# Q of two blocks by seven half-size products, with the mixed weights built in steps 7 to 14

## The chip, the cores and the metric

The kernel runs on one core of one Trainium2 chip. The metric is the device time of one execution in microseconds, as the median of several runs. Engines are named as in the profile: PE is TensorE (PEld its weight loads), DVE is VectorE, ACT is ScalarE, POOL is GpSimd, SP is SyncE, whose queue (SPq) issues every DMA here.

## What is computed

A gated cross-attention layer followed by a gated quantised linear layer, on 2048 tokens of width 512 (32 sequences of 64):

```
xn = layernorm(x)
Q = xn @ Wq.T          # 32 heads of 128
K, V = ctx @ Wk.T, ctx @ Wv.T      # 8 heads of 128, four query heads share one
P = softmax(causal(Q K^T / sqrt(128)))
x = x + tanh(g0) * ((P V) @ Wd.T)
x = x + tanh(g1) * (layernorm(x) @ dequantise(qweight).T + bias)
```

All matrix products run in f16 with each operand split in a high and a low half (HI, LO), in three passes, HI*HI, HI*LO and LO*HI.

## The kernel before, in words

The tokens form 4 blocks of 512 (`BLOCKS`, index tb), the heads 8 groups of 4 (`GROUPS`, index g). A step n = 8*tb + g, 32 in all, does the attention of one group on one block; within step n the products Q, K and V of step m = n + 1 are made too. On PE a step is written out by hand: the two score units of n, then `q_unit(m, 0..3)` (each 4 chunks of the contraction x 3 passes = 12 matmuls of 128x512), `p_transpose(n, 0)`, `k_unit(m)`, `p_transpose(n, 1)`, half of `v_unit(m)`, `av_unit(n, 0)`, `av_unit(n, 1)`, the rest of `v_unit`, then `y_unit(n, 0)`, `av_unit(n, 2)`, `y_unit(n, 1)`, `av_unit(n, 3)`, `y_unit(n, 2)`, `y_unit(n, 3)`. Steps 11 and 19 also hold four `ffn_unit`s between the Q units.

PSUM has eight banks: `pa` (2) for Q, K, V, `py` (2) for the output product, `av` (2), `ps` and `pp`. Q units alternate between the two `pa` banks, so `q_unit(m, 2)` and `(m, 3)` wait until ACT has written the HI half of the unit two before (L677) and DVE the LO half (L897, in `lo_part`). Each engine executes its own list in order, so DVE's list for a step matters: scores(n, 0), q_part 0, scores(n, 1), normalise(n, 0), q_part 1, p_part 0, normalise(n, 1), q_part 2, p_part 1, q_part 3, k_part, av_part 0 and 1, v_part, and then for j = 0 to 3: y_part(n, j) (L976, adds the output product to `xacc`), av_part(j + 2) for j < 2, and what belongs to a layernorm (`ln_bn`, `ln_stats`, `ln_norm`) or the linear layer (`ffn_zero`, `ffn_weight`) in that step.

Weights: in block 0 they are read in f32, split into HI and LO (ACT, DVE, and POOL for K, V and the output weights) and kept in DRAM (`kept_q` and so on); from step 8 on they come back from there into two buffers (`back_qkv`), the output weights `wd` into a single buffer (`back_d(n)`, which waits until the output products of step n - 1 are done). SP's queue in a step n of blocks 1 to 3: `back_d(n)`, loads of the next block's x and context, `back_qkv(m + 1)`, then DMA transposes of normalised tiles from `xh` to `xT` (`transpose_tiles`, 16 a step in four or so steps of a block), `duplicate_v(m)` and stores. POOL makes the LO halves of normalised tiles (`ln_lo`), the Newton steps of a layernorm (`ln_rstd`), `residual` and `ffn_add`.

## Time and profile before

| | us |
|---|---|
| median of 3 runs | 1057.8 (1057.64 to 1058.18) |
| the profiled execution | 1056.85 |
| its span, first to last instruction | 1054.9 |
| PE busy | 1017.7 |
| DVE busy | 682.1 |
| ACT busy | 456.6 |
| POOL busy | 233.9 |

Times in the rows count from the first instruction. Busy time says how full an engine is; what sets the end is read from the chain of waits and from the time by time view of PE. Matmuls are pipelined, so the pitch of a matmul is read as the distance of starts, not from its duration.

### The profile page before, as it was taken

Reading aid. Unit: us, or ns where it says so; the run is one execution under the profiler, and the core shown is the slowest. Engines: PE = TensorE matmul, PEld = TensorE weight load, DVE = VectorE, ACT = ScalarE, POOL = GpSimd, SP = SyncE. Lnnn points to the kernel's source line nnn. Section 1 sums busy time; section 2 is a strip of 40 time slices with the busy share of each in tenths; the row PEclk is TensorE's granted clock in tenths of the full one; section 3 lists DMA queues with packets and bytes.
Section 4 is the critical chain, followed back from the end, with each engine's and each line's share of the span. In section 5 each row is a group of like instructions: output and inputs, shape, how many; then the busy total and the mean of one; then the engine's idle time right before and its main releaser. Section 6 shows DMA issues by size and latency. Waiting matters only on the chain.

```text
span 1054.9 us, 19976 instructions
## 1 busy us (share of the span) xinstructions
PE 1017.7 (96%) x7842; PEld 569.2 (54%) x7842; DVE 682.1 (65%) x1374; ACT 456.6 (43%) x917; POOL 233.9 (22%) x245
## 2 busy tenths in 40 slices
PE   5889999999999999999999999999999999999995
PEld 3455555555555555555555554555555555555542
DVE  6856677777577666765466556755556664555678
ACT  5767676676533243333334333244433322333322
POOL 1355565465604000210002100210000300000013
PEclk9999999999999999999999999999999999999998
DMA  7757645445355632345422743333432443224111
GB/s 278 235 153 272 216 163 182 161 135 157 102 178 196 149 90 66 141 133 137 132 71 70 206 134 121 109 119 93 131 122 108 133 137 126 62 86 143 64 36 60
DMA packets 90219, 142.61 MB, mean 135 GB/s; under 512 B 31248, under 2 KB 64016, under 8 KB 79504
## 3 DMA queue, kind: packets, MB, share of 16 engines
q1 hardware_dynamic: 90128, 141.34, 42.0%
q8 instruction: 64, 1.05, 0.4%
q14 instruction: 27, 0.22, 0.1%
HBM read 94.11 MB, written 25.17 MB: 113 GB/s over the span
## 4 chain that ended last, share of the span: by engine, by line
PE 87%; DVE 7%; ACT 3%; issue 2%; DMA 1%; SPq 0%; DVEq 0%; ACTq 0%
PE pa L1295 42%; PE py L1295 30%; PE av L1408 5%; PE pp L1391 3%; PE ps L1375 2%; PE py L1466 2%; PE pp L1375 2%; DVE q L897 1%; DVE sc L943 1%; DMA raw_q<-in_wqT 1%; DVE sc L954 1%; DVE row_max L941 1%; DVE sc L937 1%; ACT q L677 1%; PE av L1442 0%
## 5 line engine op out<-in xcount | busy, mean ns | idle before, releaser
L1295 PE MATMUL pa<-xT,wq 128*128 128x512 f16 x1536 | 342.7, 379 | 9.5 <-DVE q L897 6.7
L1295 PE MATMUL py<-wd,att 128*128 128x512 f16 x1488 | 336.2, 379 | 0.8 <-issue 0.8
L1295 PEld LDWEIGHTS pa<-xT,wq 128*128 128x128 f16 x1536 | 145.8, 98 | 189.9 <-issue 22.5
L1295 PEld LDWEIGHTS py<-wd,att 128*128 128x128 f16 x1488 | 143.3, 98 | 159.1 <-issue 1.1
L677 ACT ACTIVATE q<-pa 128x512 f16<-128x512 f32 x128 | 75.7, 591 | 264.3 <-PE pa L1295 264.3
L976 DVE SCALAR_TENSOR_TENSOR xacc<-py,f_y,xacc 128x512 f32<-128x512 f32 x128 | 95.7, 747 | 125.0 <-PE py L1295 124.9
L728 ACT ACTIVATE att<-av 128x256 f16<-128x256 f32 x256 | 80.8, 384 | 145.7 <-PE av L1408 145.2
L967 DVE SCALAR_TENSOR_TENSOR att<-av,att 128x256 f16<-128x256 f32 x256 | 93.3, 416 | 67.1 <-ACT att L728 66.9
L897 DVE SCALAR_TENSOR_TENSOR q<-pa,q 128x512 f16<-128x512 f32 x128 | 87.7, 685 | 57.0 <-ACT q L677 54.2
L1295 PE MATMUL pa<-wv,cT 128*128 128x128 f16 x1536 | 96.2, 219 | 0.0
L1295 PEld LDWEIGHTS pa<-wv,cT 128*128 128x128 f16 x1536 | 89.9, 98 | 0.9
L1295 PE MATMUL pa<-cT,wk 128*128 128x512 f16 x384 | 88.1, 379 | 1.6 <-DVE q L897 1.4
L1408 PE MATMUL av<-pT,v_dup 128*128 128x256 f16 x512 | 71.6, 272 | 0.1
L897 DVE SCALAR_TENSOR_TENSOR k<-pa,k 128x512 f16<-128x512 f32 x32 | 22.1, 692 | 70.9 <-ACT k L683 70.9
L717 ACT CAST pr<-sc 128x256 f16<-128x256 f32 x64 | 32.6, 510 | 79.3 <-DVE sc L954 79.1
L721 ACT COPY pT<-pp 128x1024 f16<-128x1024 f16 x64 | 64.4, 1006 | 4.7 <-PE pp L1391 4.2
L499 POOL TENSOR_SCALAR raw_d<-raw_d,w_mul 128x512 f32<-128x512 f32 x32 | 54.3, 1697 | 21.9 <-ACT wd L672 21.9
L1295 PEld LDWEIGHTS pa<-cT,wk 128*128 128x128 f16 x384 | 36.0, 98 | 41.6 <-issue 3.3
L1408 PEld LDWEIGHTS av<-pT,v_dup 128*128 128x128 f16 x512 | 48.3, 99 | 16.7 <-issue 0.3
L556 POOL TENSOR_TENSOR xacc<-xacc,xn 128x512 f32<-128x512 f32 x8 | 10.1, 1268 | 179.7 <-DVE xacc L1104 179.7
L522 POOL TENSOR_TENSOR xh<-xn,xh 128x512 f16<-128x512 f32 x26 | 29.5, 1165 | 75.7 <-ACT xh L701 75.7
L556 POOL TENSOR_TENSOR xacc<-xacc,raw_q 128x512 f32<-128x512 f32 x4 | 5.0, 1268 | 183.6 <-DVE raw_q L1112 183.6
(131 smaller groups left out, 1060.1 us busy)
## 6 DMA issues: line engine op xcount, KB each, us to landing
wq<-kept_q SPq DMA_DIRECT2D x24, 1024.0 KB, 7.1
wd<-kept_d SPq DMA_DIRECT2D x23, 1024.0 KB, 4.8
v_dup<-v_nat SPq DMA_DIRECT2D x128, 128.0 KB, 2.4
raw_d<-in_wdT SPq DMA_DIRECT2D x8, 1024.0 KB, 10.1
kept_q<-wq SPq DMA_DIRECT2D x8, 1024.0 KB, 8.8
kept_d<-wd SPq DMA_DIRECT2D x8, 1024.0 KB, 5.4
raw_q<-in_wqT SPq DMA_DIRECT2D x7, 1024.0 KB, 5.6
wk<-kept_k SPq DMA_DIRECT2D x24, 256.0 KB, 7.3
```

The costliest lines, as they stand in the source:

```text
L499: pool.tensor_scalar(raw, raw, scale, None, ALU.mult).then_inc(w_scaled, 1)
L677: act.activation(q[:, HI, :, :, h, :], pa[h % 2][:, :].rearrange("p (b u s) -> p b u s", b=BPB, u=HALVES), ACT.Copy, scale=Q_SCALE).then_i ...
L717: act.copy(pr[:, p, :, HI, 0:keys(p)], sc[:, p, :, 0:keys(p)]).then_inc(p_hi, 1)
L721: act.copy(pT[:, :, :, p * HQ:(p + 1) * HQ], pp[:, :].bitcast(F16).rearrange("p (b h s) -> p b h s", b=BPB, h=HPG)).then_inc(pT_ok, 1)
L728: last = act.activation(att[:, HI, :, at:at + S], av[j % 2][:, bb * 256:(bb + 1) * 256].rearrange("p (h s) -> p h s", h=HPG), ACT.Copy, sc ...
L897: dve.scalar_tensor_tensor(out=out, in0=in0, scalar=scale, in1=hi, op0=ALU.mult, op1=ALU.subtract).then_inc(done, 1)
L967: last = dve.scalar_tensor_tensor(out=att[:, LO, :, at:at + S], in0=av[j % 2][:, bb * 256:(bb + 1) * 256].rearrange("p (h s) -> p h s", h= ...
L976: dve.scalar_tensor_tensor(out=acc(t), in0=py[j % 2][:, :], scalar=f_y[:, n:n + 1], in1=acc(t), op0=ALU.mult, op1=ALU.add).then_inc(y_ok, 1)
L1295: last = pe.matmul(out, stationary(a, i), moving(b, i), start=(i == 0 and (a, b) == PASSES[0]), stop=(i == count - 1 and (a, b) == PASSES[ ...
L1375: last = pe.matmul((pp, ps)[p][:, b * keys(p):(b + 1) * keys(p)], q[:, a, b, p, :, :].rearrange("p h s -> p (h s)"), k[:, c, b * S:b * S + ...
L1391: last = pe.transpose(bank16[:, b * P:(b + 1) * P], pr[:, p, b, :, :].rearrange("p c s -> p (c s)"), ident[:, :])
L1408: last = pe.matmul(av[j % 2][:, bb * 256:(bb + 1) * 256], v_dup[:, n % 2, b, c, :], pT[:, b, :, :].rearrange("p h s -> p (h s)"), start=(c ...
```

## The change

Blocks 2 and 3 (`fast(m)`, m = 16 to 31, so the Q work in steps n = 15 to 30) no longer multiply four heads one after the other. The 2x2 arrangement of two heads by two halves of the contraction, times two halves of the contraction by two halves of the tokens, is computed with Winograd's seven products. Each product `run(m, r, i)` (r: pair of heads, i = 1 to 7) is 2 chunks x 3 passes = 6 matmuls of 128x256. A step has 14 of them. Partial sums share banks: ACT copies three intermediate results out of PSUM (`copy_p1`, `copy_p5`, `copy_u2`), DVE adds three more to them (`add_11`, `add_22`, `add_12`), and the split in HI and LO is done by quadrants of 128x256.

Two sets of operands are new. The sums and differences of Wq (`ws`, kept in `kept_s`) are made one group a step in steps 7 to 14: a load of 1 MB from `in_wqT`, four tensor operations on POOL (`mix_weights`), four ACT and four DVE operations for HI and LO (`mix_hi`, `mix_lo`), and a store of 1 MB (`keep_mix`). In steps 15 to 29 `back_mix` brings them back. The sums and differences of the normalised tokens (`tT`) are made in steps 12 and 20 (`mix_norm`, `mixed_hi`, `mixed_lo`) and transposed by 32 DMA transposes in steps 13 and 14, and 21 and 22; 8 plain transposes drop out of each of these blocks' layernorms. To that end the layernorm of blocks 2 and 3 moves one step earlier (`norm_step` 3).

The last two output units of step n - 1 (`y_unit(n - 1, 2)` and `(n - 1, 3)`) move into step n between the half products for n = 15 to 30; `back_d(n)` then comes after `back_qkv`, `back_mix` and four transposes in SP's queue. In these steps `ffn_add` comes earlier on POOL, and the `ffn_zero` of the late tiles moves to after `k_part` in step 25. Small tiles share one buffer, and staging buffers are reused (`ff_raw`, `xs` and `th` in the K and V staging, `ff_int` and `ff_sum` single).

```diff
+        BANK_X, BANK_Y, BANK_Z = (pa[0], av[1]), (pa[1], pa[1]), (av[0], av[0])
...
+            def mix_weights(g):
+                pool.wait_ge(s_ld, 16 * (g + 1))
...
+                pool.tensor_tensor(a22, a22, a21, ALU.add).then_inc(s_mix, 1)
+                pool.tensor_tensor(a21, a11, a21, ALU.subtract).then_inc(s_mix, 1)
...
+                pool.tensor_tensor(a11, a22, a11, ALU.subtract).then_inc(s_mix, 1)
...
+                pool.tensor_tensor(a12, a12, a11, ALU.subtract).then_inc(s_mix, 1)
...
+                if mixing(n) is not None:
+                    pool.wait_ge(k_lo, n + 2)
+                    mix_weights(mixing(n))
```

ACT, in a fast step and, last, in steps 7 to 14:

```diff
+                if fast(m):
+                    copy_p1(m, 0)
+                    exp(n, 0)
+                    copy_p5(m, 0)
+                    copy_u2(m, 0)
+                    exp(n, 1)
+                    hi_11(m, 0)
+                    p_part(n, 0)
+                    hi_22(m, 0)
+                    hi_12(m, 0)
+                    copy_p1(m, 1)
...
+                    if mix_of(n) is not None:
+                        for t in range(TILES):
+                            mixed_hi(mix_of(n), t)
+                    if call is not None:
+                        for t in range(TILES):
+                            ln_hi(TILES * call + t, g == 0)
+                    continue
...
                 av_part(n, 2)
+                if mixing(n) is not None:
+                    mix_hi(mixing(n), (0, 1))
...
                 av_part(n, 3)
+                if mixing(n) is not None:
+                    mix_hi(mixing(n), (2, 3))
```

DVE:

```diff
+                if fast(m):
+                    scores(n, 0)
+                    scores(n, 1)
+                    add_11(m, 0)
+                    normalise(n, 0)
+                    add_22(m, 0)
+                    add_12(m, 0)
+                    lo_11(m, 0)
+                    lo_22(m, 0)
+                    lo_12(m, 0)
+                    normalise(n, 1)
+                    lo_21(m, 0)
+                    p_part(n, 0)
+                    y_late(2)
+                    p_part(n, 1)
+                    add_11(m, 1)
+                    y_late(3)
+                    add_22(m, 1)
+                    add_12(m, 1)
...
+                if mixing(n) is not None and j in (1, 2):
+                    mix_lo(mixing(n), 2 * j - 2)
+                    mix_lo(mixing(n), 2 * j - 1)
```

PE:

```diff
+                elif (r, i) == (1, 5):
+                    pe.wait_ge(c12_ok, pair_count(m, 0))
...
+                elif i == 6:
+                    pe.wait_ge(p1_ok, pair_count(m, r))
+                elif i == 7:
+                    pe.wait_ge(u2_ok, pair_count(m, r))
+                elif i == 3:
+                    pe.wait_ge(p5_ok, pair_count(m, r))
+                elif i == 4:
+                    pe.wait_ge(c22_ok, pair_count(m, r))
...
+                    elif i == 4:
+                        pe.wait_ge(t4_ld, 16 * 8 * (tb - FIRST_BLOCK + 1))
...
+                if fast(m):
+                    run(m, 0, 1)
+                    run(m, 0, 5)
+                    run(m, 0, 2)
+                    run(m, 0, 6)
+                    y_unit(n - 1, 2)
+                    run(m, 0, 7)
+                    run(m, 0, 3)
+                    run(m, 1, 1)
+                    run(m, 0, 4)
+                    run(m, 1, 5)
+                    run(m, 1, 2)
+                    run(m, 1, 6)
+                    y_unit(n - 1, 3)
+                    run(m, 1, 7)
+                    run(m, 1, 3)
+                    p_transpose(n, 0)
+                    run(m, 1, 4)
```

SP:

```diff
-                if GROUPS <= n < LAST:
+                if GROUPS <= n < LAST and not fast(m):
                     back_d(n)
...
                 if GROUPS <= m + 1 < STEPS:
                     back_qkv(m + 1)
-                if dma_tiles(n) is not None:
-                    transpose_tiles(*dma_tiles(n))
+                if fast(m + 1):
+                    back_mix(m + 1)
+                transpose_first(n)
+                if fast(m) and n < LAST:
+                    back_d(n)
+                transpose_rest(n)
                 if m < STEPS:
                     duplicate_v(m)
...
+                if mixing(n) is not None:
+                    keep_mix(mixing(n))
+                if mixing(n + 1) is not None:
+                    load_mix(mixing(n + 1))
```

## Rows read from the trace of the kernel before

**Rows 1.** The page, part 1: busy time of each engine.
```profile
PE 1017.7 (96%) x7842; PEld 569.2 (54%) x7842; DVE 682.1 (65%) x1374; ACT 456.6 (43%) x917; POOL 233.9 (22%) x245
```
**Rows 2.** The page, part 4: the chain that ended last, by engine.
```profile
PE 87%; DVE 7%; ACT 3%; issue 2%; DMA 1%; SPq 0%; DVEq 0%; ACTq 0%
```
**Rows 3.** Stretches: length, then PE, PEld, DVE, ACT, POOL busy. Step 17, step 19.
```profile
579.12:609.39 30.27, 30.22 (x238) 16.96 (x237) 16.93 (x32) 9.66 (x20) 6.02 (x5) 1.00 0.69 192
639.65:676.98 37.33, 37.33 (x274) 20.58 (x273) 23.77 (x51) 9.88 (x20) 3.42 (x3) 1.00 0.28 99
```
**Rows 4.** Time by time, PE in step 18: start, length, line, operation.
```profile
609.39 0.76 PE L1375 MATMUL pp<-k,q 128*128 128x32 f16 x24
...
610.69 10.74 PE L1295 MATMUL pa<-xT,wq 128*128 128x512 f16 x48
621.26 0.61 PE L1391 MATMUL pp<-ident,pr 128*128 128x128 f16 x8
...
626.09 1.04 PE L1408 MATMUL av<-pT,v_dup 128*128 128x256 f16 x8
626.96 1.50 PE L1295 MATMUL pa<-wv,cT 128*128 128x128 f16 x24
628.42 2.75 PE L1295 MATMUL py<-wd,att 128*128 128x512 f16 x12
631.01 0.60 PE L1408 MATMUL av<-pT,v_dup 128*128 128x256 f16 x4
```
**Rows 5.** Groups of instructions: count, busy us, mean ns of one, idle before.
```profile
L967 DVE SCALAR_TENSOR_TENSOR att<-av,att 128x256 f16<-128x256 f32 x256 | 93.3, 416 | 67.1 <-ACT att L728 66.9
L728 ACT ACTIVATE att<-av 128x256 f16<-128x256 f32 x256 | 80.8, 384 | 145.7 <-PE av L1408 145.2
L897 DVE SCALAR_TENSOR_TENSOR wq<-raw_q,w_mul,wq 128x512 f16<-128x512 f32 x32 | 31.0, 1003 | 0.2
L897 DVE SCALAR_TENSOR_TENSOR wk<-raw_k,w_mul,wk 128x512 f16<-128x512 f32 x1 | 0.8, 751 | 0.0
```
**Rows 6.** Time by time, DVE in step 18.
```profile
614.11 0.69 DVE L897 SCALAR_TENSOR_TENSOR q<-pa,q 128x512 f16<-128x512 f32 x1 [2.47 <-ACT q L677]
614.71 0.74 DVE L937 SCALAR_TENSOR_TENSOR sc<-ps,f_score,mask 128x512 f32<-128x512 f32 x1
...
616.82 0.41 DVE L950 TENSOR_REDUCE row_sum<-sc 128x8 f32<-128x256 f32 x1
...
617.85 0.68 DVE L897 SCALAR_TENSOR_TENSOR q<-pa,q 128x512 f16<-128x512 f32 x1
...
618.93 0.69 DVE L950 TENSOR_REDUCE row_sum<-sc 128x8 f32<-128x512 f32 x1
...
620.50 0.68 DVE L897 SCALAR_TENSOR_TENSOR q<-pa,q 128x512 f16<-128x512 f32 x1
```
**Rows 7.** Time by time, DVE and POOL in steps 8 and 9.
```profile
305.90 0.69 DVE L943 TENSOR_TENSOR sc<-sc,row_max 128x512 f32<-128x512 f32 x1
...
336.16 1.28 DVE L943 TENSOR_TENSOR sc<-sc,row_max 128x512 f32<-128x512 f32 x1
...
331.76 5.14 POOL L550 TENSOR_TENSOR xacc<-xacc,ff_rows 128x512 f32<-128x512 f32 x4 [1.48 <-DVE ff_rows L1096]
```
**Rows 8.** Time by time, DVE in step 10 (its first score matmul is at 360.19).
```profile
364.92 0.69 DVE L897 SCALAR_TENSOR_TENSOR q<-pa,q 128x512 f16<-128x512 f32 x1 [0.22 <-ACT q L677]
```
**Rows 9.** Time by time, POOL in steps 8 and 11.
```profile
319.65 0.20 POOL L543 TENSOR_TENSOR rstd<-rs_t,rs 128x4 f32<-128x4 f32 x1
...
421.96 1.27 POOL L556 TENSOR_TENSOR xacc<-xacc,xn 128x512 f32<-128x512 f32 x1 [85.06 <-DVE xacc L1104]
```
**Rows 10.** SP's queue: 16 transposes of step 18; the reload of `wd`, us to landing.
```profile
611.68 20.97 SPq L400 DMA_TRANSPOSE xT<-xh  x16
...
wd<-kept_d SPq DMA_DIRECT2D x23, 1024.0 KB, 4.8
```
**Rows 11.** Time by time, ACT at the end of step 20: HI halves of a layernorm.
```profile
702.80 2.19 ACT L701 ACTIVATE xh<-xn 128x512 f16<-128x512 f32 x4
```

More of the change, by code:

```diff
@@ L26 @@
 STEPS = BLOCKS * GROUPS
+HB = BT // 2
+HK = D // 2
 HI, LO = 0, 1
@@ L568, in _ @@
                     split_wv(1)
+                if mix_of(n) is not None:
+                    mix_norm(mix_of(n))
                 if call is not None:
                     ln_rstd(call)
+                if ffn_of(n) is not None and fast(n + 1):
+                    for t in range(ffn_of(n) * TILES, (ffn_of(n) + 1) * TILES):
+                        ffn_add(t)
                 if tb == 0:
@@ L579, in _ @@
                         residual(t)
-                if ffn_of(n) is not None:
+                if ffn_of(n) is not None and not fast(n + 1):
                     for t in range(ffn_of(n) * TILES, (ffn_of(n) + 1) * TILES):
@@ L821, in _ @@
                     ctx_squares(tb + 1, squares_done(g + 2) + 2 if tb == 0 else squares_done(GROUPS))
+                if mix_of(n) is not None:
+                    for t in range(TILES):
+                        mixed_hi(mix_of(n), t)
                 if call is not None:
@@ new lines, in _ @@
+                if fast(m):
[12 more added lines that the diff above has]
+                    y_late(2)
+                    p_part(n, 1)
+                    add_11(m, 1)
+                    y_late(3)
+                    add_22(m, 1)
+                    add_12(m, 1)
+                    lo_11(m, 1)
+                    lo_22(m, 1)
+                    lo_12(m, 1)
+                    lo_21(m, 1)
+                    if ffn is not None:
+                        ffn_scaled(t0)
+                    k_part(m)
+                    if g == 1 and tb == BLOCKS - 1:
+                        for t in LATE:
+                            ffn_zero(t)
+                    if ffn is not None:
+                        ffn_scaled(t0 + 1)
+                        ffn_scaled(t0 + 2)
+                    if call is not None and g == 0:
+                        ln_stats(call)
+                    av_part(n, 0)
+                    av_part(n, 1)
+                    if ffn is not None:
+                        ffn_scaled(t0 + 3)
+                    v_part(m)
+                else:
+                    scores(n, 0)
+                    if n == 0:
+                        for h in range(2, HPG):
+                            split_wq(1, h)
+                    q_part(m, 0)
+                    scores(n, 1)
+                    normalise(n, 0)
+                    q_part(m, 1)
+                    if n == 0:
+                        weight_scale(1, slice(3, 4))
+                        step_factors(n)
+                    if ffn is not None:
+                        ffn_scaled(t0)
+                    p_part(n, 0)
+                    normalise(n, 1)
+                    q_part(m, 2)
+                    if ffn is not None:
+                        ffn_scaled(t0 + 1)
+                    p_part(n, 1)
+                    q_part(m, 3)
+                    if ffn is not None:
+                        ffn_scaled(t0 + 2)
+                        ffn_scaled(t0 + 3)
+                    k_part(m)
+                    if call is not None and g == 0:
+                        ln_stats(call)
+                    av_part(n, 0)
+                    av_part(n, 1)
+                    v_part(m)
@@ L1204, in _ @@
                 for j in range(TILES):
-                    if n < LAST - 1:
+                    if n < LAST - 1 and not (deferred(n) and j >= 2):
                         y_part(n, j)
@@ L1220, in _ @@
                         ffn_zero(t0 + j)
-                    if g == 1 and tb == BLOCKS - 1:
-                        ffn_zero(LATE[j])
                     if prep:
```

458 lines of the change are left out of this document (365 added, 93 removed).

## The prediction

> **What bounds the kernel now.** I read the busy shares first: PE 1017.7 of 1054.9 us, DVE 65% [rows 1]. The chain of waits says the same, 87% on PE [rows 2]. Then the stretches of one step: an ordinary step of blocks 1 to 3 takes 30.27 us of which PE is busy 30.22, and step 19, with the linear layer, 37.33 of 37.33 [rows 3]. So a microsecond of matmul taken out is a microsecond gained, as long as no wait takes its place. The time by time view gives the pitches [rows 4]. A 12-matmul unit of 128x512 takes 631.01 - 628.42 = 2.59 us, 216 ns each; eight of 128x256 take 626.96 - 626.09 = 0.87 us, 109 ns each. Four Q units would be 4 x 2.59 = 10.36; they take 621.26 - 610.69 = 10.57. The missing 0.21 is a wait: `q_unit(m, 3)` needs the LO half of unit 1, which DVE finishes at 617.85 + 0.68 = 618.53 [rows 6], 9.14 after the step's start at 609.39, when unit 3 is due at 9.07. DVE is thus level with PE in the first third of each step, although it is busy only 16.93 of 30.27 us [rows 3]. What it has in reserve is the 2.47 us idle before 614.11 [rows 6].
>
> **What the change removes.** Per fast step 48 matmuls at 10.57 us become 14 x 6 = 84 at 109 ns = 9.16 us: 1.41 us less. 16 steps (n = 15 to 30), of which step 19 has no 0.21 wait: 22.4 us. The pitch is from the `av` product, the same form (f16, 128x256, weights changed at every matmul), so I see no reason for another. From a page of the Trainium skill another sum would follow: TensorE: Matmul & The Clock Gate, Back-to-back issue gap, states a sustained spacing of about 81 ns at 128 columns and 131 at 512, with weight loads in the stream; by it (an estimate, midway in columns some 98 ns) 84 short products would cost more than 48 long ones, 8.2 against 6.3 us, and the change would lose. The trace disagrees at both ends I can read, 216 ns at 512 and 109 at 256 [rows 4], and the measurement decides.
>
> **The ordinary fast step, placed by hand.** Half product = 0.66 us. From the step's start on PE: scores to 1.30; products 1, 5, 2 to 3.27, 6 to 3.92; y2 to 6.51; 7 and 3 to 7.82; 1' to 8.48; 4 to 9.13; 5', 2', 6' to 11.10; y3 to 13.69; 7', 3', the transpose to 15.44; 4' to 16.10. The rest is as before, so the step ends at 28.86. DVE starts its scores at 1.6, later than before, since av_part(3) (ends 1.65) no longer has y2 and y3 behind it. scores 0 takes 1.4, scores 1 616.82 - 614.71 = 2.11, an addition like one L967 0.36 to 0.42, normalise 0 617.85 - 616.82 = 1.03 [rows 5, 6]: idle at 6.45. Product 7 is read at 7.37, `add_22` is done at 7.75, product 4 wants it at 8.48. DVE may be 1.5 us late there. Second chain: `add_12` 8.40, three LO quadrants at 0.36, normalise 1 620.50 - 618.93 = 1.57, lo_21, p_part 0, y2 (0.7), p_part 1, `add_11'` end near 13.3; y3 arrives at 13.9, `add_22'` is done at 14.95, wanted at 15.44. So 0.3 us is spare after y3 and 0.6 before. ACT's eight quadrants and six copies at 0.38 [rows 5] fit: `copy_u2'` done at 13.0, wanted at 13.69. I take 0 for the ordinary step, with 0 to 0.5 as bounds (the upper if each of the 10 additions and LO quadrants in the chain takes 0.42 with gaps, not 0.36). Nothing hides more than that.
>
> **Where waits appear: fast steps.**
> - Steps 15 and 23, first products on a new block. One DMA transpose holds SP's queue 20.97 / 16 = 1.31 us [rows 10]. Step 22 has 4 + 16 of them, step 21 as many, steps 13 and 14 20 each. Adding up SP's queue (reloads 2.1, four transposes 5.3, `back_d` held until y3 at 13.9, 16 x 1.33, the V copies 2.6), step 22 begins at 9.1 in its own time, and the last transpose is issued at 9.1 and lands at 10.6 in step 23, where product 4 wants it at 8.5: 2.1 us. By the same sum step 15 waits 1.4. Bounds 0 and 5 together.
> - Step 22: `back_d` issued at 16.9 lands 4.8 later [rows 10] at 21.7, wanted at 22.8; beside transposes it may take 7: 0.5 taken, 0 to 1.5.
> - Steps 17, 21, 25: four ACT operations on layernorm tiles take 2.19 to 2.6 us [rows 11]; they now come after av_part(3) (0.86) with no y2 and y3 as cover and ahead of `copy_p1`, done then at 3.7 for a product 6 due at 3.27: 0.6 each.
> - Step 20: step 19's DVE list ends with ctx, four normalisations, four `ffn_zero` (0.7 each), so its scores start 3.1 us late, 1.6 over what is spare, and POOL's `ffn_add` beside it: 2.1. Steps 16, 24 (two statistics around y3) 0.3 each; step 19 0.2; step 25, four `ffn_zero` ahead of av_part: 0.7.
> Sum: 1.4 + 2.1 + 0.5 + 1.8 + 2.1 + 0.6 + 0.2 + 0.7 = 9.4, bounds 3 and 18.
>
> **Where waits appear: steps 7 to 14.** POOL's four operations of one group are 4 x 1.3 = 5.2 us [rows 9], the DVE's four between 0.75 and 1.0 each [rows 5]; no POOL work lies beside them, so 0.75 with overlap, 2.7 us. After y1 and y2 DVE has about as much idle time, so in steps 7, 13 and 14 this costs nothing (if the 1.0 held, 1 us each). It isn't free where the list is full:
> - Step 8: POOL ends the Newton steps at 319.85 [rows 9], and only then mixes, to 325.3. ACT waits for that ahead of av_part(3), so DVE has it at 328.3, and y3 due at 326.74 waits: 1.7 us.
> - Step 9: POOL's `residual` moves later over DVE's scores. With POOL active, L943 takes 1.28 in place of 0.69 [rows 7]: 0.6 more. So says a rule of the Trainium skill too (SBUF — State Buffer, Who interferes with whom): DVE with two SBUF inputs and a reading GpSimd exclude each other; the trace agrees with its 1.28.
> - Step 10: the first Q part on DVE came at 364.92 with 0.22 idle before it [rows 8]. To the `ffn_weight` work of step 9 come the 2.7 and, by the earlier layernorm, two statistics (1.3). DVE's Q part 0 ends 8.0 into the step where unit 2 is due at 6.5 (1.5), and part 1 ends at 11.8 for unit 3 at 10.6 (1.2): 2.5 more than now.
> - Step 11, with its four linear units as cover: 0.4. Steps 11 and 12: `ln_norm` before y1, then `ffn_add` and `mix_norm` of POOL (eight operations at 1.27) over DVE's scores: 1.5.
> Sum 6.7, bounds 2 and 11. The DMA traffic, some 32 MB more, stays behind other work: the loads are issued most of a step ahead.
>
> **The sum.** 22.4 - 9.4 - 6.7 = 6.3 us. The profiled span of 1054.9 becomes 1048.6; 1.95 lies around it in that execution (1056.85), and the median is another 0.95 higher: 1057.8 - 6.3 = 1051.5.
>
> **The rivals.**
> - The waits overlap. A step in which PE waited gives DVE, SP and POOL time too, so the waits of neighbouring steps aren't a sum. With the lower bounds 3 and 2 the gain is 17.4: 1040.4. For it: 8 of my 11 fast waits are under 1 us. Against: those of steps 8, 10, 20, 23 have different causes. Chance 0.22, within 1040 to 1048.
> - SP's queue. 20 transposes take 26 us of a 28.9 us step, and if transposes slow down beside the 1 MB loads, `back_d` and the last transposes are late in all steps with transposes, ten steps at 0.5 to 1 us: gain near 0, 1056 to 1060. Against: in step 18 wq, wk, wv and 16 transposes ran together at 1.31. Chance 0.15.
> - The other side: DVE sets the pace of the fast steps. Mechanism: the wait of product 4' for `add_22'`, behind everything DVE does between y2 and y3. It decides from 0.3 us of lateness on; if additions and quadrants take 0.48 and each semaphore hop 0.1 more, lateness is 1 to 1.5 a step, 16 to 24 us: 1061 to 1075. For it: DVE rises from 17 to about 20 us busy in a step of 28.9, and the present 0.21 wait shows how it gets level with PE. Against: L967's pairs show 0.36. It turns into a loss at 0.4 us a step. Chance 0.15.
> - The half products don't get the pitch per column: a cost per matmul, and not per column, holds them, say at 160 ns, halfway between 109 and 216. Then 84 x 0.16 = 13.4 us, 2.9 more than now in each of 16 steps, and with the 16 us of waits 1120. The `av` row speaks against it [rows 4]. Chance 0.02; the page of the Trainium skill named above points this way.
>
> **How the numbers follow.** Forecast 0.46 (gain 3 to 10, 1048 to 1055). About 0.2% is what a measurement of this kernel tells from no change. Faster: 0.46 + 0.22 and some of the queue case, 0.70. Same: most of the queue case, 0.14. Slower: 0.15 and 0.02 less rounding, 0.16. The range from 1040 to 1060 leaves out the DVE case and the weight loads; within it lie 8 in 10.
>
> **What would show it.** Right: 84 half products at 109 ns in 9.2 us of PE; ordinary steps 26 to 30 of 28.9 us; waits of PE above 1 us only in steps 8, 10, 12, 15, 20 and 23, the last on DMA. Wrong: a DVE wait before product 4' in every fast step, steps 13 and 14 longer than 30.3, or `wd` as a releaser of y0. If all of 22 us arrives, my DVE lateness is overestimated; if step 30 isn't shorter than 29.5, the pitch or the ordinary step is wrong.

## The result and the profile after

The changed kernel takes 1075.6 us (median of 4 runs, 1073.5 to 1076.3), the kernel before 1058.0 beside it: ratio 1.0162, interval 1.0144 to 1.0180. It is slower by 1.6%, where 1051.5 was forecast and 1060 was the upper end. The profiled execution of the changed kernel took 1073.51, its span is 1071.7.

The page of the changed kernel: the span, part 1 (busy us, share, instructions), the granted clock in 40 slices, and the chain that ended last.

```profile
span 1071.7 us, 22269 instructions
...
PE 1005.0 (94%) x8418; PEld 626.8 (58%) x8418; DVE 757.7 (71%) x1566; ACT 522.4 (49%) x1117; POOL 307.8 (29%) x293
...
PEclk9999999999999999999989999999999999999998
...
PE 63%; DVE 16%; SPq 10%; ACT 4%; issue 4%; DMA 2%; DVEq 0%; ACTq 0%
```

PE lost only 12.7 us of busy time against [rows 1], although 22.4 us of matmul went. Some of its matmuls ran at a lower clock (5.2 us in steps 12, 15 and 22, below), and busy time grows a little in a step that waits even at the full clock: 29.39 us in step 17 for the 28.86 of step 18. The chain fell from 87% on PE [rows 2] to 63%; 16% now is DVE and 10% SP's queue, which had 0%.

The next view gives stretches: length, then PE, PEld, DVE, ACT, POOL busy with counts, granted clock, DMA share, GB/s. Steps 17 and 18.

```profile
593.84:624.72 30.88, 29.39 (x275) 20.39 (x273) 22.57 (x44) 14.61 (x38) 10.68 (x8) 1.00 0.64 203
624.72:653.58 28.86, 28.86 (x274) 20.55 (x272) 20.61 (x46) 12.30 (x30) 0.00 (x0) 1.00 0.52 164
```

Step 18 takes 28.86 us, all of it PE, where it took 30.27 [rows 3]: that is the forecast for an ordinary fast step, to the hundredth. The 22.4 us therefore did arrive. Step 17, with POOL at work for 10.7 us, takes 2.0 more. So I compared the length of each step (from score start to score start) with its length without waits. Those are 30.27 for a step of blocks 1 to 3, 28.86 for a fast one, 37.32 for step 11, 36.14 for step 19, in which the trace shows no wait, and 25.09 for step 14, whose last two output units went into step 15. Step 9 is compared with its 30.85 in the kernel before, as the forecast did. A measured wait contains the lower clock behind it.

| waits, us | forecast | measured |
|---|---|---|
| step 8 | 1.7 | 1.4 |
| step 9 | 0.6 | 1.8 |
| step 10 | 2.5 | 2.6 |
| step 11 | 0.4 | 0.3 |
| step 12 | 1.5 | 4.7 |
| step 14 | 0 | 0.6 |
| step 15 | 1.4 | 11.1 |
| step 17 | 0.6 | 2.0 |
| step 20 | 2.1 | 3.8 |
| step 22 | 0.5 | 5.9 |
| step 23 | 2.1 | 1.3 |
| step 25 | 1.3 | 3.0 |
| steps 16, 19, 21, 24 | 1.4 | 0.7 |
| sum | 16.1 | 39.2 |

39.2 less 22.4 is a loss of 16.8 us, as the two spans have it; the medians show 17.6. Of the 23.1 us by which the waits exceed the forecast, 9.7 are one step. PE in step 15 (its scores start at 524.73), time by time: start, length, and in brackets the idle time before and its releaser.

```profile
526.75 0.82 PE L1768 MATMUL pa<-xT,wq 128*128 128x256 f16 x6 [0.56 <-issue]
528.65 0.81 PE L1768 MATMUL pa<-raw_q 128*128 128x256 f16 x6 [1.08 <-DMA raw_q<-raw_kv]
...
534.51 0.82 PE L1768 MATMUL av<-xT,wq 128*128 128x256 f16 x6
542.12 1.44 PE L1768 MATMUL pa<-raw_q,wq 128*128 128x256 f16 x6 [6.79 <-DMA raw_q<-raw_kv]
543.35 1.49 PE L1768 MATMUL pa<-raw_q 128*128 128x256 f16 x6
544.63 1.49 PE L1768 MATMUL av<-xT,wq 128*128 128x256 f16 x6
545.91 0.89 PE L1768 MATMUL av<-raw_q 128*128 128x256 f16 x6
```

`raw_q<-raw_kv` is a mixed transpose. PE waits 6.79 us for the last of them, and the three products behind the wait come 1.23, 1.28 and 1.28 us apart, while the others keep 0.655. The granted clock of that stretch (542.12 to 545.91) is 0.50, which is the 1.2 GHz level in place of 2.4; it costs another 1.9 us. After it, it is 1.00 again. SP's queue of the same stretch:

```profile
439.10 5.08 SPq L561 DMA_DIRECT2D out_x<-xacc  x4
...
448.89 20.97 SPq L477 DMA_TRANSPOSE xT<-xh  x16
469.95 3.10 SPq L453 DMA_DIRECT2D v_dup<-v_nat  x4
...
478.26 10.07 SPq L477 DMA_TRANSPOSE xT<-xh  x8
488.51 16.71 SPq L489 DMA_TRANSPOSE raw_q<-raw_kv  x12
505.32 2.60 SPq L453 DMA_DIRECT2D v_dup<-v_nat  x4
...
513.82 27.02 SPq L489 DMA_TRANSPOSE raw_q<-raw_kv  x20
```

The 56 transposes take 74.8 us, 1.34 each, and with what stands between them the queue works from 444 to 541 with no gap above 0.6 us. Before that its stores wait for POOL's `ffn_add`. Step 22 shows the same queue with the reload of `wd` in it: SP first, then PE.

```profile
765.04 5.04 SPq L489 DMA_TRANSPOSE raw_d<-raw_kv  x4
770.17 0.53 SPq L440 DMA_DIRECT2D wd<-kept_d  x1
770.81 23.66 SPq L489 DMA_TRANSPOSE raw_d<-raw_kv  x16
```
```profile
778.30 4.36 PE L1693 MATMUL py<-wd,att 128*128 128x512 f16 x12 [4.23 <-DMA wd<-kept_d]
795.70 0.82 PE L1768 MATMUL pa<-raw_d,wq 128*128 128x256 f16 x6 [1.10 <-DMA raw_d<-raw_kv]
```

The reload is issued at 18.95 us of the step and is usable 8.1 us later, beside transposes that take 1.48 each. The 12 matmuls behind the wait take 4.36 us in place of 2.75, again at the lower clock level for most of it (granted 0.59 from 778.30 to 782.30).

My theory after this reading: some 18 us are SP's queue, which the mixed transposes fill (step 15, 22, 23), and the rest are DVE: operations with two operands in SBUF slowed by POOL, and lists that are too long in steps 8 to 12. The rivals are named with each run.

### The profile page after: what moved, and what is told of

Same layout as the page of the kernel before. It is cut to its first block, busy times and chain, and to the rows that moved or that the text cites. A ratio compares the mean times of both kernels' runs of the same rounds, so it can differ in the third digit from the quotient of the medians.

```text
span 1071.7 us, 22269 instructions
## 1 busy us (share of the span) xinstructions
PE 1005.0 (94%) x8418; PEld 626.8 (58%) x8418; DVE 757.7 (71%) x1566; ACT 522.4 (49%) x1117; POOL 307.8 (29%) x293
## 4 chain that ended last, share of the span: by engine, by line
PE 63%; DVE 16%; SPq 10%; ACT 4%; issue 4%; DMA 2%; DVEq 0%; ACTq 0%
PE py L1693 23%; PE pa L1693 20%; SPq L489 8%; PE pa L1768 5%; PE av L1872 4%; PE av L1768 4%; DVE q L1194 2%; PE pp L1850 2%; PE py L1930 2%; SPq L477 1%; PE ps L1834 1%; DVE xacc L1323 1%; PE pp L1834 1%; DVE xacc L1451 1%; DVE sc L1290 1%
## 5 line engine op out<-in xcount | busy, mean ns | idle before, releaser
L1693 PE MATMUL py<-wd,att 128*128 128x512 f16 x1488 | 340.7, 380 | 7.9 <-DMA wd<-kept_d 5.0
L1693 PE MATMUL pa<-xT,wq 128*128 128x512 f16 x768 | 173.6, 381 | 15.8 <-DVE q L1194 13.9
L1693 PEld LDWEIGHTS pa<-xT,wq 128*128 128x128 f16 x768 | 72.9, 98 | 107.9 <-issue 25.8
L871 ACT ACTIVATE q<-pa 128x512 f16<-128x512 f32 x64 | 37.7, 589 | 81.7 <-PE pa L1693 81.7
L738 POOL TENSOR_TENSOR xacc<-xacc,raw_kv 128x512 f32<-128x512 f32 x12 | 17.6, 1482 | 207.8 <-DVE raw_kv L1463 177.0
L915 ACT COPY pT<-pp 128x1024 f16<-128x1024 f16 x64 | 64.2, 1003 | 4.7 <-PE pp L1850 4.2
L687 POOL TENSOR_TENSOR small<-rs 128x4 f32<-128x4 f32 x18 | 4.6, 258 | 210.3 <-DVE rs L1348 209.4
L1872 PEld LDWEIGHTS av<-pT,v_dup 128*128 128x128 f16 x512 | 48.3, 99 | 16.9 <-issue 0.3
L907 ACT ACTIVATE sc<-sc 128x256 f32<-128x256 f32 x64 | 33.4, 521 | 45.4 <-DVE sc L1290 45.4
L1194 DVE SCALAR_TENSOR_TENSOR q<-pa,q 128x512 f16<-128x512 f32 x64 | 43.7, 683 | 13.1 <-ACT q L871 12.5
```

Of the source, the lines that this page charges most:

```text
L871: act.activation(q[:, HI, :, :, h, :], pa[h % 2][:, :].rearrange("p (b u s) -> p b u s", b=BPB, u=HALVES), ACT.Copy, scale=Q_SCALE).then_i ...
L907: act.activation(sc[:, p, :, 0:keys(p)], sc[:, p, :, 0:keys(p)], ACT.Exp).then_inc(exp_ok, 1)
L915: act.copy(pT[:, :, :, p * HQ:(p + 1) * HQ], pp[:, :].bitcast(F16).rearrange("p (b h s) -> p b h s", b=BPB, h=HPG)).then_inc(pT_ok, 1)
L1194: dve.scalar_tensor_tensor(out=out, in0=in0, scalar=scale, in1=hi, op0=ALU.mult, op1=ALU.subtract).then_inc(done, 1)
L1693: last = pe.matmul(out, stationary(a, i), moving(b, i), start=(i == 0 and (a, b) == PASSES[0]), stop=(i == count - 1 and (a, b) == PASSES[ ...
L1872: last = pe.matmul(av[j % 2][:, bb * 256:(bb + 1) * 256], v_dup[:, n % 2, b, c, :], pT[:, b, :, :].rearrange("p h s -> p (h s)"), start=(c ...
```

## Experiments

**The mixed transposes left out.** Left out are the 64 transposes and all waits for them; the seven products read the plain tokens, so Q comes out wrong, but PE's work is the same. If the queue is the cause, the 64 transposes alone explain steps 15, 22 and 23; the rival is DVE.

```diff
             def transpose_mixed(tb, some):
 
+                return
...
-                b = xT[:, par, :, :, :] if i in (1, 2, 3) else tT[par]
+                b = xT[:, par, :, :, :]
```

> Left out: the 64 DMA transposes of the mixed tokens (32 for each of blocks 2 and 3) and the waits for them; the seven products read the plain tokens instead, so their values are wrong but their work is the same. Theory A (SP's queue is the cause of the DMA waits): in the changed kernel's trace step 15 is 11.1 us, step 22 5.9 and step 23 1.3 longer than the 28.86 of an ordinary fast step, 18.3 in all, with the transposes' wait (6.8 + 1.1), the reload of wd (4.2) and a lower clock behind them. All of it goes: 1075.6 - 18.3 = 1057, steps 15, 22 and 23 between 28.9 and 30. Rival B (DVE is late there too, the wait on DMA only covers it): step 15 starts with DVE 2.7 us late from the weights' LO parts, and at least 1.2 us of step 15 stay; if the DVE is worse than that, steps 15 and 23 stay above 31 and the time is 1062 to 1070.

Measured: 1056.5 us, ratio 0.9983 (0.9971 to 0.9996). Step 15 takes 29.86, steps 22 and 23 take 28.87 and 28.86, step 14 takes 25.09; all others are as in the changed kernel, to 0.04. In step 15 one wait is left:

```profile
535.11 0.83 PE L1767 MATMUL pa<-xT,wq 128*128 128x256 f16 x6 [0.68 <-DVE junk L1231]
```

The loads of the mixed weights are still in the queue here. So the mixed transposes cost 19.1 us by the medians and 17.9 by the four steps, as waits and by the clock behind them. Without any of them the change gains only 1.5 to 2 us of 22.4: the other half of the loss is elsewhere.

**The stores a step later.** The queue's long run begins with four stores that wait for POOL's `ffn_add`. If they move behind the transposes, these start earlier.

```diff
-                if ffn_of(n) is not None:
-                    for t in range(ffn_of(n) * TILES, (ffn_of(n) + 1) * TILES):
+                if n > 0 and ffn_of(n - 1) is not None:
+                    for t in range(ffn_of(n - 1) * TILES, (ffn_of(n - 1) + 1) * TILES):
                         store(t)
```

> Same work; the four stores of steps 11 and 19 stand one step later in SP's queue, behind the transposes of steps 12 and 20. Theory A: in step 12 the queue then waits only for the weights' LO parts (ready at 439.6) and its transposes start 4.6 us earlier, in step 20 about 6 us earlier. Of step 15's wait of 6.8 about 2.2 is left and its lower clock goes, step 22's wait of 4.2 for wd goes, together 10 to 12 us less: 1064. Rival C (the queue is full anyway, 20 transposes a step at 1.33, so it catches up with the same lateness): no more than 3 us less, 1073.

Measured: 1074.5 us, ratio 1.0152 (1.0123 to 1.0182). My expectation of 1064 fell and the rival's 1073 held. This execution's step 12 starts at 435.88, the changed kernel's at 433.79, so times are compared from there. The 16 transposes start 10.2 us into step 12 in place of 15.1: the head start of 4.9 us that I expected was there. The next row of transposes starts only 2.0 us earlier (42.5 in place of 44.5), since the four stores, 2.2 us of queue, now stand between them.

```profile
446.11 21.05 SPq L477 DMA_TRANSPOSE xT<-xh  x16
467.26 2.60 SPq L453 DMA_DIRECT2D v_dup<-v_nat  x4
469.90 2.16 SPq L561 DMA_DIRECT2D out_x<-xacc  x4
...
478.39 10.07 SPq L477 DMA_TRANSPOSE xT<-xh  x8
```

The last 20 end 104.9 us after the start of step 12 in place of 107.1. PE still waits 6.63 us for them, and steps 14 and 15 together are 1.6 us shorter, while 22 and 23 are 0.6 longer. Reordering alone mends little in a full queue.

**One part alone, twice.** First the weights are mixed, stored and fetched by nobody, and Q is made as before (no fast step, no sums of the tokens). Then the reverse: seven half products in the fast steps, but no sums of weights; they read the plain weights.

```diff
         def fast(m):
-            return FIRST_FAST <= m < STEPS
+            return False
```

> Q of all blocks by whole heads as before; kept from the change: the sums and differences of the weights in steps 7 to 14 (made and stored, never used) and the layernorm one step earlier; left out: the mixing of tokens. Theory A: steps 8 to 12 cost what they cost in the changed kernel, 1.4 + 1.8 + 2.6 + 0.3 and of step 12's 4.7 perhaps 3 (the token sums on POOL are missing), so 9 us over before: 1067, and steps 13 to 30 at 30.3. Rival D (this work is hidden behind PE and the cost sits in the fast steps): within 2 us of 1057.8.

```diff
         def mixing(n):
...
-            return g if 0 <= g < GROUPS else None
+            return None
```

> The fast steps and the mixing of tokens as changed; left out: the sums and differences of the weights in steps 7 to 14, their loads and stores; the second set of weights comes back from the plain kept weights, so the values are wrong. Theory A: steps 8 to 11 return to the lengths of before (30.3, 30.9, 30.3, 37.3; 6 us less), step 12 keeps a part of its 4.7 (POOL's additions beside DVE's scores; 1 to 2 left), and SP's queue reaches step 15 some 5 us less late, 5 to 7 us less there: 1075.6 - 6 - 3 - 6 = 1060.6. Rival D: the first steps stay as long and only fast steps change: above 1068.

Measured: 1069.2 (1.0102, 1.0073 to 1.0132) and 1057.1 (0.9995, 0.9980 to 1.0011). With the weights mixed alone steps 8 to 12 take 31.69, 32.64, 32.88, 37.66 and 34.85, the same as in the changed kernel to 0.15; from step 13 on all but steps 20 and 25 are 30.27 or 37.32. Step 12's wait was the surprise: I had put it down to the sums of the tokens, and it is there without them. Without the mixing, steps 8 to 12 are 30.28, 30.86, 30.28, 37.32 and 31.02, and step 15 waits 2.6 us for a transpose in place of 6.8:

```profile
527.74 0.82 PE L1767 MATMUL pa<-raw_q,wq 128*128 128x256 f16 x6 [2.59 <-DMA raw_q<-raw_kv]
```

The queue's transposes begin 10.0 us into step 12 in place of 15.1, and from the first of them to the end of the last it needs 86.4 us in place of 92.0, with the loads and stores of the mixed weights gone from it. PE, whose step 12 is 4.0 us shorter, takes back a part of this. Steps 22 and 23 together are 65.54 us, against 64.93 with the mixing: in those steps there are no such loads and stores in either kernel, and the queue is just as late.

**POOL's additions made narrow.** `residual` and `ffn_add` work on 4 columns of 512, so that POOL is busy for much less time at the same places. The rest of the output then lacks the bias and the linear layer's result. If contention on SBUF is the cause, steps 9, 12, 17, 20 and 25 get shorter; if DVE's lists are too long, nothing does.

```diff
-                pool.tensor_tensor(acc(t), acc(t), part, ALU.add).then_inc(out_pool, 1)
+                pool.tensor_tensor(acc(t)[:, 0:4], acc(t)[:, 0:4], part[:, 0:4], ALU.add).then_inc(out_pool, 1)
```

> As the changed kernel, but POOL's residual and ffn_add work on 4 of 512 columns, so the bias and the linear layer's result are missing from the rest of the output; all instructions, their order and waits stay. Theory A (DVE operations with two operands in SBUF are held up by POOL's): steps 9, 12, 17, 20 and 25 were 1.4 + 1.8, 4.7, 2.0, 3.8 and 3.0 over their length without waits; step 17 falls to 0.5, step 12 to 2, step 20 to 2.6, step 25 to 1.5, step 9 by 0.5: some 8 us less, and the stores, done sooner, let SP's queue start 5 us earlier in steps 12 and 20, worth 1 to 3 more: 1065. Rival B (DVE's own list is too long there, POOL is no part of it): at most 1 us less in these steps: 1073 or more.

Measured: 1060.0 us, ratio 1.0015 (1.0000 to 1.0029). Step 9 0.8 shorter, 12 0.9, 17 1.6, 20 1.7, 25 1.7. DVE and POOL in step 17 of the changed kernel, and then DVE at the same place with narrow additions:

```profile
602.57 1.03 DVE L1194 SCALAR_TENSOR_TENSOR q<-p,q 128x256 f16<-128x256 f32 x1
603.52 2.89 DVE L1194 SCALAR_TENSOR_TENSOR q<-junk,q 128x256 f16<-128x256 f32 x2
```
```profile
600.57 5.56 POOL L732 TENSOR_TENSOR xacc<-xacc,ff_rows 128x512 f32<-128x512 f32 x4
```
```profile
600.75 0.42 DVE L1194 SCALAR_TENSOR_TENSOR q<-p,q 128x256 f16<-128x256 f32 x1
601.09 0.75 DVE L1194 SCALAR_TENSOR_TENSOR q<-junk,q 128x256 f16<-128x256 f32 x2
```

A LO quadrant takes 0.42 us alone and 1.03 to 1.45 beside POOL. The seven products copy partial results to SBUF, so three of the four quadrants now have both operands there; before, the split read Q from PSUM. That is how the change made DVE more sensitive to POOL. The form with an operand in PSUM isn't slowed: `q<-pa,q`, of twice the width, keeps its 0.68 in the middle of POOL's 437.37 to 443.83.

```profile
442.63 0.68 DVE L1194 SCALAR_TENSOR_TENSOR q<-pa,q 128x512 f16<-128x512 f32 x1
```

The steps give 6.8 us in all, the span 12.0. Step 22 gains 4.7 us and step 23 waits 4.7 longer, so the two together stay at 64.92: when `wd` comes sooner, PE meets the same late transposes one step later. As for the span, the other 5.2 lie behind the start of step 31, where the last linear layer's own `residual` and `ffn_add` are narrow too (50.0 us to the end in place of 55.3). That part says nothing on the change. The medians differ by 15.6, of which the profiled executions show 11.3; the rest is the spread between executions.

**The LO halves of the mixed weights by ACT.** It takes the four `mix_lo` a step off DVE. What ACT writes is the scaled weight, not its LO half.

```diff
-                        mix_lo(mixing(n), 2 * j - 2)
-                        mix_lo(mixing(n), 2 * j - 1)
...
+                    for h in range(HPG):
+                        act.activation(ws[mixing(n) % 2][:, LO, h, :, :], raw_s[:, h, :].rearrange("p (k n) -> p k n", k=KC),
+                                       ACT.Copy, scale=w_mul[:, mixing(n), 0:1]).then_inc(s_lo, 1)
```

> As the changed kernel, but in steps 7 to 14 the LO parts of the mixed weights are written by ACT as plain copies behind the HI parts (their values are wrong), and DVE has none of these four operations a step. Theory A (step 10's 2.6 us are DVE's list: mix_lo 2.7 us and two more statistics behind the linear weights): step 10 falls to within 0.5 us of 30.27, step 9 from 32.6 to 31, step 12 from 35.0 to 33, step 8 stays at 31.7, as it hangs on POOL and ACT: 6 us less: 1069. Rival C (the earlier layernorm and POOL make these steps long): steps 9, 10 and 12 shrink by under 1 us together, 1074.

Measured: 1072.0 us, ratio 1.0126 (1.0101 to 1.0151). Step 10 falls from 32.88 to 30.28 and step 11 to 37.32: there it is DVE's list. Step 12 falls by 2.4 of its 4.7. Step 14 takes 32.12, since `wd` comes 5.2 us late, and step 15 2.7 less. Step 9 became longer (33.50 in place of 32.63). The trace shows how: ACT's four extra operations (2.55 us) delay its HI halves of the layernorm, so POOL's `ln_lo` starts 0.65 us into step 9, where it had started 1.80 before it, and the last row of `ffn_rows` on DVE takes 1.64 us in place of 0.68:

```profile
335.17 1.64 DVE L1446 SCALAR_TENSOR_TENSOR ff_rows<-ff_rows 128x512 f32<-128x512 f32 x1
```
```profile
332.52 5.32 POOL L670 TENSOR_TENSOR xh<-xn,xh 128x512 f16<-128x512 f32 x4 [6.26 <-ACT xh L895]
```

DVE's list of step 11 in the changed kernel, POOL beside it, and what PE makes of it:

```profile
431.61 3.22 DVE L1194 SCALAR_TENSOR_TENSOR raw_q<-raw_d,w_mul,raw_q 128x512 f16<-128x512 f32 x2
...
436.31 3.31 DVE L1194 SCALAR_TENSOR_TENSOR raw_q<-raw_d,w_mul,raw_q 128x512 f16<-128x512 f32 x2
```
```profile
431.28 6.12 POOL L670 TENSOR_TENSOR xh<-xn,xh 128x512 f16<-128x512 f32 x4 [6.37 <-ACT xh L895]
437.37 6.46 POOL L738 TENSOR_TENSOR xacc<-xacc,raw_kv 128x512 f32<-128x512 f32 x4
```
```profile
443.45 7.05 PE L1693 MATMUL pa<-xT,wq 128*128 128x512 f16 x24 [3.02 <-DVE q L1194]
```

A `mix_lo` takes 1.6 us here; two take 1.41 where POOL is still, as at 395.36. The four cost 6.5 us, not 2.7, ahead of step 12's scores on DVE. PE waits 3.02 us, and the 24 matmuls behind the wait take 6.89 us to the next start in place of 24 x 0.216 = 5.18: step 12's 4.7 us are 3.0 of wait and 1.7 of lower clock (granted 0.75 over the 24). No single edit took all of it away: without `mix_lo` 2.3 us are left, with narrow additions 3.8.

**Half of the mixed transposes by PE.** The tiles 0 and 1 are transposed by PE in 2 x 8 short matmuls and copied out by ACT; SP keeps 32 of 64. All of the work is done.

```diff
+                for c in (HI, LO):
+                    for i in range(KC):
+                        at = (c * KC + i) * P
+                        last = pe.transpose(bank16[:, at:at + P], th[:, t, c, i * P:(i + 1) * P], ident[:, :])
+                last.then_inc(tm_mm, 1)
```

> Complete work. Of the 32 DMA transposes of mixed tokens in each of blocks 2 and 3, the 16 of the first two tiles are done on PE (8 transposes into one av bank and one ACT copy, one tile in each of steps 13, 14, 21 and 22). Theory A (SP's queue, at 1.32 us a transpose, is what makes steps 15, 22 and 23 long): without all 64 the kernel took 1056.5; 32 fewer take 21 us off the queue in each block, more than the 8 us that it was late, so the DMA waits go as they did there, and PE gains 4 x 0.45 us of work: 1058.5, step 15 at 29.9, steps 22 and 23 at 28.9 (step 22 29.3). Rival C (the queue stays full, since reloads and V copies wait on one another in it): a wait on DMA above 1 us is left in step 15 or 22: 1061 or more.

Measured: 1060.3 us, ratio 1.0019 (1.0006 to 1.0031). Steps 15, 22 and 23 take 29.87, 30.01 and 28.87. The 32 transposes taken over cost PE 0.45 us in each of four steps, and the kernel gains 15.3 us net. This settles the queue: with the same data by another way its loss is all but gone.

**POOL and stores a step later as well.** To the last kernel are added: the stores a step later; `residual`, `ffn_add` and the sums of the tokens later on POOL, behind the last LO quadrants; `mix_hi` after av_part 3; the late `ffn_zero` in step 26.

```diff
-                if g == 0 and tb > 0:
+                if g == 1 and tb > 0:
+                    pool.wait_ge(k_lo, n + 2)
                     for t in range((tb - 1) * TILES, tb * TILES):
                         residual(t)
```

> Complete work: the former kernel, and POOL's and ACT's work put where DVE is not in its first third. residual a step later and behind k_part; ffn_add in the step after, behind k_part (its stores a step later too); the token sums of step 12 behind the fourth Q unit; the HI parts of the mixed weights behind av_part 3; the late ffn_zero in step 26. Theory A (placement of POOL beside DVE's scores and LO quadrants): of the former's waits step 8's 1.4, 1.2 of step 9, 3 of step 12, 2.0 of step 17, 1.5 of step 20, 2.5 of step 25 go, 11 us: 1047 to 1049, faster than the kernel before. Rival B (the waits hang on the length of DVE's list, not on POOL): 1055 or more.

Measured: 1055.5 us, ratio 0.9957 (0.9941 to 0.9973), faster than both kernels but 6 us short of my expectation. The profiled execution is the slowest of the seven (1059.0, the fastest took 1053.7), so a fall of the clock that it shows need not be in the median. Steps 12, 17 and 25 take 32.27, 29.22 and 29.23, as wanted. Three places didn't follow. Step 8 stayed at 31.70, so the order on ACT, my mechanism of the prediction, wasn't its cause. Step 20 stayed at 32.72; DVE and POOL ahead of its scores, then PE:

```profile
682.08 4.00 DVE L1467 SCALAR_TENSOR_TENSOR xacc<-ff_rows,small,xacc 128x512 f32<-128x512 f32 x3
```
```profile
681.25 5.84 POOL L671 TENSOR_TENSOR xh<-xn,xh 128x512 f16<-128x512 f32 x4 [30.42 <-ACT xh L897]
```
```profile
688.42 1.08 PE L1783 MATMUL pa<-raw_q,raw_d 128*128 128x256 f16 x6 [2.02 <-ACT junk L945]
```

And step 22 took 33.04, for `wd` stands behind four transposes; behind a wait of 1.99 us the clock was at the lower level (granted 0.57 from 767.05 to 771):

```profile
767.05 4.45 PE L1708 MATMUL py<-wd,att 128*128 128x512 f16 x12 [1.99 <-DMA wd<-kept_d]
```

**Room for DVE in three places.** One edit for each of these.

```diff
+                if mixing(n) == 1:
+                    pool.wait_ge(q_lo, 4 * n + 8)
+                    mix_weights(1)
                 if call is not None:
                     ln_rstd(call)
...
-                transpose_first(n)
+                if fast(m) and g != 6:
+                    transpose_first(n)
                 if fast(m) and n < LAST:
                     back_d(n)
+                if not fast(m) or g == 6:
+                    transpose_first(n)
...
+                    if g == 2 and tb == 2:
+                        ffn_zero(4 + j)
```

> The complete work, as in the kernel of e8 (half of the mixed transposes by PE, stores and three of POOL's lists a step later), with three more edits, each against one wait that was left there. (1) Step 8: POOL makes the sums of the weights of group 1 ahead of the norm's reciprocal roots, from the moment when the last quadrant of Q is written, and not beside DVE's four ln_norm. Theory (two engines on SBUF operands slow each other, ln_norm 0.91 each in place of 0.48): the four take 1.91 us again and step 8 goes from 31.70 to 30.3. Rival (the engines aren't what slows it, DVE's list is too long): 31.7 stays. (2) Step 20's start: the four ffn_zero of block 1 go from step 19 to step 18, so that they don't lie beside POOL's ln_lo ahead of the scores; theory: step 20, which was 32.72 with 2.0 of wait and a fall of the clock behind it, takes 29.0 to 29.5; rival: the scores of step 20 stay late by DVE's ln_norm, 31 or more. (3) Step 22: SP issues the reload of wd ahead of four transposes (4.98 us of its queue) and no longer behind them; theory: the wait of 1.99 us on wd and the half clock behind it go, step 22 from 33.04 to 29.9; rival (the transfer is slowed by the transposes behind it, wherever it stands): 31.5 to 33. Sum by the theory 1.4 + 3.4 + 3.1 = 7.9 us under e8's 1055.5: 1047.6, range 1046 to 1050, ratio to the kernel before 0.990. If all three rivals hold: 1054 or more.

Measured: 1049.1 us (5 runs, 1047.0 to 1050.3), ratio 0.9914 (0.9900 to 0.9927). Step 8 takes 31.04, step 22 29.36 and step 20 28.90; step 9 took 32.22, 0.4 more. The profiled execution is the fastest of its five, that of the kernel with POOL and stores later the slowest of its seven: they differ by 12 us and the medians by 6.3, so the steps overstate what the three edits give. Of the 3.8 us of step 20, 1.75 came back in step 19 (37.90), where DVE is now late with the scores: the four `ffn_zero` take 3.0 us of its list wherever they stand. The four `ln_norm` of step 8, first in the changed kernel beside POOL's sums, then in this one, where POOL has ended by 317.4:

```profile
322.56 3.65 DVE L1400 TENSOR_SCALAR xn<-xacc,mv,small 128x512 f32<-128x512 f32 x4
```
```profile
322.34 1.26 POOL L702 TENSOR_TENSOR raw_d<-raw_d 128x512 f32<-128x512 f32 x1
323.69 1.33 POOL L704 TENSOR_TENSOR raw_d<-raw_d 128x512 f32<-128x512 f32 x1
```
```profile
323.13 1.91 DVE L1422 TENSOR_SCALAR xn<-xacc,mv,small 128x512 f32<-128x512 f32 x4
```
```profile
316.14 1.27 POOL L708 TENSOR_TENSOR raw_d<-raw_d 128x512 f32<-128x512 f32 x1
```

With that the 1.27 us wait of step 8 is gone. The 0.77 us that are left are a new one: POOL's sums now lie beside DVE's short operations of `ln_stats`, one of which takes 1.24 us in place of 0.17, and PE's first output unit waits for av_part 1 behind them:

```profile
316.19 1.24 DVE L1367 TENSOR_SCALAR small<-small 128x4 int32<-128x4 int32 x1
```
```profile
318.55 1.67 PE L1716 MATMUL py<-wd,att 128*128 128x512 f16 x7 [0.73 <-DVE att L1336]
```

Its page, against [rows 1, 2] and the rows of the changed kernel above:

```profile
PE 999.1 (96%) x8450; PEld 626.6 (60%) x8450; DVE 747.8 (72%) x1566; ACT 525.7 (50%) x1121; POOL 302.4 (29%) x293
...
PE 75%; DVE 17%; ACT 4%; issue 3%; DMA 1%; SPq 0%; DVEq 0%; ACTq 0%
```

SP's queue has left the chain. The edits could hardly have helped the kernel before, whose steps 8 to 30 wait only 0.6 us in all (step 9) beyond what every step has; but no run has them in that kernel, and 1.1 us of the profiled gain lie behind the start of step 31, where the change does nothing. With that reserve the 9 us are the change's own gain, less what it still costs: steps 8 to 13 wait 7.6 us more than before and the fast steps some 4.6.

## Why the prediction was wrong, point by point

**What holds.** The gain of 22.4 us: a half product takes 0.655 us, 109 ns a matmul, and an ordinary fast step 28.86, with 0 taken for waits. The rivals on the pace of DVE and on a cost per matmul are thereby refuted: steps 18, 21, 26 to 29 wait for nothing. That the measured time lies at the end of the range of the DVE rival (1061 to 1075) is chance; by its own 16 to 24 us that range should begin at 1067. Of the waits the sizes of steps 8, 10, 11, 16, 19 and 24 were right to 0.3 us. That of step 23 was right to 0.8, by luck (below). For step 10 the cause was right too (its wait vanished with `mix_lo` off DVE). Step 25's 0.93 us for four `ffn_zero` ahead of av_part was there too, where 0.7 was taken.

**Step 15: 1.4 taken, 11.1 measured.** The step that failed first is the placing of step 15 in SP's sum. I gave step 14 its 30.27 us (I named "longer than 30.3" as a sign of being wrong there); but its last two output units moved into step 15, and it takes 25.09 without waits. So everything on PE's side was due 5.2 us earlier against the queue. I had seen the move as work that only changes place. The second error was the queue itself: counted from the start of step 14, my forecast has the last transpose usable at 40.2 us (30.27 + 8.5 + 1.4), and it was at 43.1. That makes 1.4 + 5.2 + 2.9 = 9.5 us behind the time at which PE could have used it. PE spent 2.6 of these in shorter waits in steps 14 and 15 and 6.79 on the last transpose; that 1.4 + 5.2 alone comes near 6.79 is chance. To the 9.5 come 1.9 of lower clock behind the long wait, which wasn't in my sum at all. About 1.0 of step 15's 11.1 stays without any mixed transpose.

**The queue's bounds, 0 and 5 for steps 15 and 23 together.** They measured 12.4. The queue case of my rivals named the right place, not the right mechanism: it had slower transposes cost 0.5 to 1 us in ten steps, and the loss fell in three. The argument against it, transposes at 1.31 us beside loads [rows 10], was true of step 18 and didn't touch the point, that the queue has no slack left in four steps in a row. I gave the case 0.15 and at most 1060. My own sign of being wrong, `wd` as a releaser of the first output unit, did appear, in steps 14, 15 and 22.

**Steps 22 and 23: 2.6 taken, 7.2 measured.** In step 22 the issue of `wd` at 16.9 was forecast, 18.95 came; 4.8 to 7 us to landing were forecast [rows 10], 8.1 came. Each was off by 1 to 2 us, and then a wait of 4.23 took the clock down for the 12 matmuls behind it, 1.6 us more. The 16 transposes behind `wd` took 1.48 us each, not 1.33, another 2.4: with the 2.05 of the later issue the last one came 4.5 us later than forecast, which is the whole of the excess. How it divides between the two steps hangs on `wd`: it is 5.9 and 1.3 here, 1.2 and 6.0 with narrow additions, and 7.2 both times. So the 2.1 for step 23 came out near the 1.3 only because step 22 had already waited.

**Contention of DVE and POOL.** I priced it from one row, L943 at 1.28 in place of 0.69 [rows 7], and used it in step 9 only. Four kinds of operation that I had at full speed fell under it: the LO quadrants (0.42 to 1.45), `mix_lo` (0.7 to 1.6), `ffn_zero` (0.74 to 1.09, and 1.33 in the kernel with POOL and stores later) and `ln_norm` (0.48 to 0.91). [rows 5] had the sign: the operation that `mix_lo` repeats takes 1003 ns there in the mean, and I took 0.75. Terms that were mis-sized where it acts: step 12 by 3.2 us, the clock included ("no POOL work lies beside them", I wrote of `mix_lo`; there are 12.6 us of it), step 17 by 1.4, step 20 by 1.7, step 25 by 1.7, step 9 by 1.2. With narrow additions steps 17, 20 and 25 lose 5.0 of their 8.8 us of waits, steps 9 and 12 only 0.8 and 0.9; that the rest of step 12 is `mix_lo` beside POOL's `ln_lo` and `ffn_add` is read from the trace and not shown by a run of its own. The 0.6 that I took in steps 17, 21 and 25 for ACT came to 0.2, 0 and 0.2. The Trainium skill has a rule that covers all four (SBUF — State Buffer, Who interferes with whom): an operation of DVE with two SBUF inputs contends with a GpSimd operation that reads SBUF, and so does a `tensor_scalar` in a two-port mode. The trace agrees in time, 3.65 against 1.91 us for four `ln_norm`; which mode they ran in it doesn't show. I had cited the rule and not gone through the list of new operations with it.

**Step 8: right size, wrong cause.** I had ACT wait for POOL ahead of av_part 3. With that order changed the step stayed at 31.70; with POOL's sums moved away from `ln_norm` the wait on DVE ahead of the last output unit went, 1.27 us, and a new one of 0.73 ahead of the first came, since the sums now lie beside `ln_stats`.

**The clock.** No term of my sum had it. It cost 1.9 us in step 15, 1.7 in step 12 and 1.6 in step 22.

**Open.** Why the queue's last transposes before step 15 came 2.9 us later than I had placed them, since my sum for that step isn't written out. And how much each of the last three edits gives in a median execution.

## What to carry to other kernels

Work that moves from the end of one step to the next moves the due times of every queue by its length, even where PE's total stays: redo the sum of each queue against the shortened step, and price a serial queue by its length over all neighbouring steps. When a change spills partial results from PSUM to SBUF, list each operation that now has both operands in SBUF with what POOL does beside it, as each may take twice its time or more. A long wait of PE was paid a second time in the clock behind it (4.23 us of wait, 1.6 more), which many short ones were not. And steps of two executions are compared from the start of a step: here step 0 alone began between 37.1 and 41.7 us.
